# An attention stack on one core: projections moved a few slots, copies put around an exponential, splittings re-ordered

## The reference

```python
# l0: 20 heads of width 8, keys and values from ctx_2048 (512 rows of 256),
# text keys 0..76 and the remaining "ip" keys with their own weights and softmax
q = x @ Wq.T;  k, v = text @ Wk.T, text @ Wv.T;  k_ip, v_ip = ip @ Wk_ip.T, ip @ Wv_ip.T
x = (attend(q, k, v) + attend(q, k_ip, v_ip)) @ Wo.T + bo + x
# a1: self attention, 20 heads of width 64
n = layer_norm(x);  x = x + attention(n, n)
# a2: cross attention, 20 heads of width 64, here with ctx_2048 as the context
n = layer_norm(x);  x = x + attention(n, ctx_2048)
# ff
x = geglu(layer_norm(x)) + x
```

## Time and profile before

| what | value |
|---|---|
| median of 3 runs | 1513.89 us (1512.29 to 1514.84) |
| the profiled execution, its own time | 1517.58 us |
| its span, first to last instruction | 1515.8 us |
| mean granted TensorE clock | 0.997 |
| busy TensorE, VectorE, ScalarE, GpSimd | 98%, 71%, 51%, 29% |
| busy TensorE's weight loads | 77% |

### The profile page before, as it was taken

The page is one execution under the profiler, slowest core; times in us unless marked ns, Lnnn a source line. Parts: engine busy times, 40 slices in busy tenths (PEclk is TensorE's granted clock), DMA queues, the critical chain, the costliest instruction groups (busy, mean ns, idle before and its releaser), DMA issues.

```text
span 1515.8 us, 40910 instructions
## 1 busy us (share of the span) xinstructions
PE 1480.4 (98%) x17984; PEld 1168.8 (77%) x17984; DVE 1080.2 (71%) x1509; ACT 779.6 (51%) x1079; POOL 445.2 (29%) x393
## 2 busy tenths in 40 slices
PE   9999999999999999998999999999999999999999
PEld 6566566567888888887787888887888888778799
DVE  6778878866777777776677676766767677676666
ACT  4667666764554455654344444444444444443344
POOL 4433346431222223542122122222222222222210
PEclk9999999999999999999999999999999999999999
DMA  4322231300000200011010100101010030000000
GB/s 142 117 62 63 62 113 43 97 3 23 2 2 2 98 2 6 2 30 29 23 30 1 30 2 2 29 2 30 2 29 2 2 75 2 1 2 2 1 14 22
DMA packets 27212, 45.53 MB, mean 30 GB/s; under 512 B 7392, under 2 KB 15520, under 8 KB 26656
## 3 DMA queue, kind: packets, MB, share of 16 engines
q1 hardware_dynamic: 27040, 42.96, 9.7%
HBM read 29.51 MB, written 1.31 MB: 20 GB/s over the span
## 4 chain that ended last, share of the span: by engine, by line
PE 84%; ACT 5%; DVE 5%; POOL 2%; issue 1%; SPq 1%; DMA 0%; ACTq 0%; POOLq 0%; DVEq 0%
PE a_pj L1022 7%; PE a_pj L1010 6%; PE a_pj L534 5%; PE l_px L1695 5%; PE a_pv L1044 4%; PE a_px L1044 4%; PE l_pst L1593 4%; PE a_px L1062 3%; PE a_px L577 3%; PE a_pscore L950 3%; PE a_pj L543 3%; PE ff_ph L2187 3%; PE a_pst L971 2%; PE a_px L563 2%; PE a_pv L563 2%; ACT l_probs L1834 2%
## 5 line engine op out<-in xcount | busy, mean ns | idle before, releaser
L1296 POOL TENSOR_TENSOR a_key_sum<-a_probs 128x512 f32<-128x512 f32 x120 | 166.0, 1387 | 455.4 <-ACT a_probs L1121 455.4
L1203 DVE TENSOR_REDUCE a_negmax<-a_pscore 128x2 f32<-128x1024 f32 x160 | 195.5, 1222 | 94.4 <-PE a_pscore L950 94.0
L1121 ACT ACTIVATE a_probs<-a_pst 128x1024 f32<-128x1024 f32 x160 | 164.0, 1025 | 156.1 <-PE a_pst L977 155.5
L1965 DVE TENSOR_REDUCE l_negmax<-l_pscore 128x2 f32<-128x154 f32 x320 | 202.7, 684 | 49.4 <-PE l_pscore L1578 48.4
L1834 ACT ACTIVATE l_probs<-l_pst 128x1024 f32<-128x1024 f32 x160 | 164.1, 1026 | 80.7 <-PE l_pst L1593 79.8
L761 POOL TENSOR_TENSOR a_key_sum<-a_probs 128x1024 f32<-128x1024 f32 x40 | 96.8, 2421 | 223.8 <-ACT a_probs L625 223.8
L701 DVE TENSOR_REDUCE a_negmax<-a_pscore 128x4 f32<-128x1024 f32 x80 | 97.6, 1220 | 35.3 <-PE a_pscore L492 35.2
L1022 PE MATMUL a_pj<-a_wv_hi,a_ct 128*128 128x256 f32 x640 | 111.9, 287 | 1.0
L713 DVE RECIPROCAL a_recip<-a_pv 128x256 f32<-128x256 f32 x40 | 70.3, 1757 | 43.3 <-PE a_pv L568 43.3
L625 ACT ACTIVATE a_probs<-a_pst 128x1024 f32<-128x1024 f32 x80 | 81.9, 1023 | 37.2 <-PE a_pst L518 37.2
L1228 DVE RECIPROCAL a_recip<-a_pv 128x256 f32<-128x256 f32 x40 | 70.2, 1755 | 42.5 <-PE a_pv L1053 42.5
(11 more groups left out here) (259 smaller groups left out, 3638.4 us busy)
## 6 DMA issues: line engine op xcount, KB each, us to landing
l_ct<-in_ctx_t SPq DMA_DIRECT2D x8, 512.0 KB, 3.9
l_k_stack<-l_k_hi SPq DMA_DIRECT2D x64, 64.0 KB, 2.1
a_ct<-in_ctx_t SPq DMA_DIRECT2D x8, 512.0 KB, 4.6
a_ct<-in_ctx_t SPq DMA_DIRECT2D x16, 256.0 KB, 5.5
l_q_stack<-l_q_hi SPq DMA_DIRECT2D x80, 32.0 KB, 1.9
a_raw_wv<-in_a_wv SPq DMA_DIRECT2D x2, 1280.0 KB, 8.6
l_x<-in_x_t SPq DMA_DIRECT2D x8, 256.0 KB, 3.8
l_k_stack<-l_k_lo SPq DMA_DIRECT2D x32, 64.0 KB, 2.1
```

The lines of the kernel that those rows point to most:

```text
L1121: nc.scalar.activation(probs[:, 2 * i:2 * i + 2, 2 * n:2 * n + 2, :], pst[:].rearrange("p h (k q) -> p h k q", k=2), ACT.Exp, scale=SCALE) ...
L1203: nc.vector.tensor_reduce(to, pscore[:], AX.X, ALU.max, negate=True).then_inc(max_done, 1)
L1296: nc.gpsimd.tensor_tensor(key_sums[n][:, two], probs[:, two, 2 * n, :], probs[:, two, 2 * n + 1, :], ALU.add).then_inc(half_summed, 1)
L1965: last = nc.vector.tensor_reduce(to[:, :, k], pscores[s % 2][:, :, keys], AX.X, ALU.max, negate=True)
```

## The change

- EARLY: queries of batch 1 are projected in part (2, 3) and no longer (2, 1); the keys' rest in (3, 3) and no longer (2, 3). FILLED gets six matmuls at (2, 1). The fill at (3, 3) falls away, since a projection is there now.
- ScalarE: the hi copy of the keys' rest is made in the part that projects it; the lo copy stays in part 0 of the next step, behind the exponential. Both were there. This holds for all seven batches that have it.
- VectorE: a2's opening for step d-1 is called between the two parts of step d of a1, and no longer behind rest(d-1). Only openings 27 and 39 hold anything; 39 stays in its place.
- The step from a1 to a2, ScalarE: opening(39) rounds context parts 0 and 1 only; opening(40), behind the exponential of own part 0, parts 2 and 3; opening(41), behind the queries' rounding, makes sel.
- VectorE: low_context(0, 0) comes before low_queries(0), low_context(0, 1) in part 1, behind the second maximum.
- TensorE: keys(0) waits for c_ready at its first row that uses the low context (row 8, and again at 9 to 11) and no longer at row 6.

```diff
--- before.py
+++ after.py
@@ -1001,11 +1001,11 @@
                 elif u == 0:
                     pe.wait_ge(c_ready, 4 * (b + 1))
                 pe.wait_ge(q_split, d + 1)
-            if d == 0 and part == 1:
-                pe.wait_ge(c_ready, 4)
             half = len(C_ROWS) // 2
             for k in range(part * half, (part + 1) * half):
                 hw, hc, s = C_ROWS[k]
+                if d == 0 and hc == 1:
+                    pe.wait_ge(c_ready, 4)
                 for t in range(2):
                     last = mm(pj[:, t, :], wk[hw][OWN[t], s, u * P:(u + 1) * P], cts[b % 2][OWN[t], hc, s, :],
                               start=k == 0, stop=k == len(C_ROWS) - 1)
@@ -1153,13 +1153,13 @@
             if d in (33, 34):
                 act.wait_ge(loaded[2], 16)
                 copy(wv[0][:, d - 33], raws["wv"][:, d - 33]).then_inc(w_hi, 1)
-            if d == 39:
+            if d == 41:
                 for i in range(2):
                     nc.scalar.activation(sel[:, i, :], ident[:, i:i + 1].broadcast_to([P, P]), ACT.Identity,
                                          bias=ident[:, D1 + i:D1 + i + 1]).then_inc(sel_set, 1)
-            if d == 39:
-                for s in range(4):
-                    high_context(0, s)
+            if d in (39, 40):
+                for s in range(2):
+                    high_context(0, 2 * (d - 39) + s)
 
         def part(d, s):
             if here(d - 2):
@@ -1254,12 +1254,11 @@
                 if d == 1 and s == 0:
                     dve.wait_ge(negmax_zeroed, 1)
                 maximum(d - 1, s)
+            if d == 0 and s < 2:
+                low_context(0, s)
             if s == 0:
                 if here(d):
                     low_queries(d)
-            if (d, s) == (0, 1):
-                for k in range(2):
-                    low_context(0, k)
             if s == 1 and norm_at(d, LN_SPLIT):
                 ln.dve_lo(dve, norm_at(d, LN_SPLIT), nt)
             if s == 1 and d > 1 and norm_at(d, LN_STATS):
@@ -1419,8 +1418,8 @@
 
 
     EARLY = {(0, 0): ("v3", 0), (0, 1): ("ip", 1), (0, 2): ("v0", 1), (1, 0): ("v1", 1), (1, 1): ("text", 1),
-             (2, 1): ("q", 1), (2, 3): ("rest", 1), (3, 1): ("v2", 1), (4, 1): ("v3", 1)}
-    FILLED = {(0, 3): 8, (1, 2): 4, (1, 3): 8, (2, 0): 4, (2, 2): 4}
+             (2, 3): ("q", 1), (3, 1): ("v2", 1), (3, 3): ("rest", 1), (4, 1): ("v3", 1)}
+    FILLED = {(0, 3): 8, (1, 2): 4, (1, 3): 8, (2, 0): 4, (2, 1): 6, (2, 2): 4}
     PLAN = {(0, 1): "ip", (0, 3): "text", (1, 1): "q", (1, 3): "rest", (2, 3): "v0", (3, 1): "v1", (3, 3): "v2",
             (4, 1): "v3"}
 
@@ -1864,9 +1863,6 @@
                 for u in range(GROUPS):
                     wait(act, stacked[u], MOVES[u] * m)
                 pairs = [(q_n["hi"][:], q_n["lo"][:], pj[:].rearrange("p (i q) -> p i q", i=2))]
-            elif what == "rest":
-                wait(act, stacked[GROUPS - 1], MOVES[GROUPS - 1] * m)
-                pairs = [(rest_n["hi"][:], rest_n["lo"][:], pj[:])]
             elif what in ("ip", "text"):
                 for u in range(GROUPS - 1):
                     wait(act, stacked[u], MOVES[u] * (m - 1))
@@ -1879,6 +1875,15 @@
                 return
             take_values(int(what[1]), m, pj).then_inc(pj_read, 1)
 
+        def take_rest(m, half):
+
+            if half == "hi":
+                act.wait_ge(pj_ready, pj_uses["rest", m] + 1)
+                wait(act, stacked[GROUPS - 1], MOVES[GROUPS - 1] * m)
+                copy(rest_n["hi"][:], pj[:])
+            else:
+                copy(rest_n["lo"][:].bitcast(FP32), pj[:]).then_inc(pj_read, 1)
+
         def take_values(kt, m, bank):
 
             vm = vs[m % 2]
@@ -1912,8 +1917,10 @@
 
 
             if s == 0 and projected(t - 1, 3) and projected(t - 1, 3)[0] == "rest":
-                take(*projected(t - 1, 3))
-            if projected(t, s) and projected(t, s)[0] not in ("out", "s0", "rest"):
+                take_rest(projected(t - 1, 3)[1], "lo")
+            if projected(t, s) and projected(t, s)[0] == "rest":
+                take_rest(projected(t, s)[1], "hi")
+            elif projected(t, s) and projected(t, s)[0] not in ("out", "s0"):
                 take(*projected(t, s))
 
         return dict(begin=begin, part=part)
@@ -2471,7 +2478,11 @@
             cross["opening"](S1 - 1)
             for d in range(2):
                 own["part"](S1 + d, 0)
+                if d == 0:
+                    cross["opening"](S1)
                 cross["part"](d, 0)
+                if d == 0:
+                    cross["opening"](S1 + 1)
                 own["part"](S1 + d, 1)
                 for s in range(1, 4):
                     cross["part"](d, s)
@@ -2515,9 +2526,11 @@
             own["rest"](3)
             for d in range(4, S1):
                 own["part"](d, 0)
+                if d < S1 - 1:
+                    cross["opening"](d - 1)
                 own["part"](d, 1)
                 own["rest"](d)
-                cross["opening"](d)
+            cross["opening"](S1 - 1)
             for d in range(2):
                 own["part"](S1 + d, 0)
                 cross["part"](d, 0)
```

## The result

The changed kernel takes 1507.82 us (median of 8 runs, 1505.48 to 1508.77) against 1516.52 for the kernel before, timed beside it (1512.29 to 1517.82): a ratio of 0.9942, with a 95% interval of 0.9932 to 0.9953. That is 8.7 us won, where 8.0 were forecast.

A forecast was written before the change was run, and what follows sets the result against it. TensorE, busy 98%, was taken as the bound, so only its idle or low-clock time could change. Terms -2.4 - 1.35 - 5.1 + 0.7 = -8.15, say -8.0 us, from median 1513.89 gave 1505.9; range 1502.9 to 1510.6.

The forecast's parts named there:

- second and third gap: TensorE idle: 1.35 us at 592.62 for a maximum; 1.14 then 2.73 us at the step from a1 to a2.
- first gap: First layer's step 2: TensorE idle 2.12 us before the turning of the maxima, then some 6 us at half speed.
- Part 1: Keys' rest, one copy before and one after the exponential: five waits and a sixth change, 2.4 us won.
- Part 2: VectorE's low rows of wq behind a1's first maximum: the 1.35 us gap closes; bounds 1.1 and 1.55.
- Part 3: Step from a1 to a2: idle and low clock go, queries wait longer; 5.1 us won if VectorE precedes GpSimd.
- The rival order: At the a1 to a2 step, GpSimd's key sum starts before VectorE's second context subtraction; about 2.3 us won, chance 0.30.
- Part 4: New slots for queries, rest and fills in the first steps: new wait at step 5, 0.7 us net cost.
- Cover 1.2: At step 5's first projection, only 1.2 us of the slots' gain counts, since GpSimd's split ends near 56.5.
- Price 1.9: Clock falls again behind the new wait of about 2.3 us at step 5, costing 1.9 us.
- B: GpSimd ahead of VectorE at the a1 to a2 step: -5.35 us, 1508.5; chance 0.30.
- C: Slots cost 1.8, copies win 1.2, wq move 1.1, GpSimd ahead: -2.8 us, 1511.1; chance 0.17.
- D: Hi copy waits for each batch's last stack, delaying exponentials: slower, 1514 to 1518 us; chance 0.03.

The follow-up runs named there:

- p4_slots: Kernel before with only the new slots of the first steps (queries, keys' rest, fills); 1517.27 us, span 1515.5.
- p1_halves: Kernel before with only the hi copy of the keys' rest moved into the part that projects it; 1514.28 us, span 1512.5.
- p2_wq: Kernel before with only VectorE's opening of the next layer moved between the two parts of a1's step; 1514.70 us, span 1512.9.
- b_xs_last: Kernel before with the xs loads and three small loads moved behind the second batch's last stack; 1517.39 us, span 1515.6.
- a_xs_later: Changed kernel with the eight xs loads and three small loads moved behind the second batch's third stack; span 1508.6 us.
- after_again: Changed kernel unaltered, timed again as reference for the moved loads; 1507.39 us, ratio 0.9937 to the kernel before, span 1504.4.
- a_fill20: Changed kernel with 20 useless matmuls in front of step 5's first projection, where TensorE waited for GpSimd; span 1505.6 us.
- a_key_sum_first: Changed kernel with GpSimd's memset behind its key sum, so the sum starts ahead of VectorE's second context subtraction; span 1506.9 us.

## Why the prediction was right, step by step

- **What bounds.** Right. To within 0.3 us, all that was won lies in TensorE's second and third gap, the copies' waits and the stretch of low clock behind the third gap; what the first gap gave was spent again at step 5.
- **Part 1, predicted -2.4.** Measured -2.5 in the change, -2.7 alone. The hi copy found the idle time in front of the exponential; L1739's wait is gone. TensorE's lead grew by 0.30 us at the change that is followed by fills (forecast 0.24) and by 0.46 to 0.50 at each of the other five (0.45); 0.2 of it was lost again near 300 us, in the change only.
- **Part 2, predicted -1.35.** -1.6 from a1's first projection to a2's queries, in the change (377.1 us to 375.5) and alone (375.5). The 0.25 beyond the gap of 1.35 has no row that explains it. The 1.5 us more that it brought alone is the hidden price of the clock and not part 2's.
- **Part 3, predicted -5.1.** -5.1 both ways, and in the forecast order: VectorE 0.24 us ahead of GpSimd, against 0.15 rolled. The wait for the queries was 0.93 us, forecast 0.8. The rival order was overpriced: 1.9 us, measured, against 5.1 - 2.3 = 2.8. It charged a wait of 2.2 us, which was 1.63, and clock as well, but the clock held. One reading behind this part was wrong: low_queries, 0.69 us, was taken as a subtraction with GpSimd silent, but GpSimd's pair of 2.52 us from 706.33 was under way at 708.21. One input of low_queries lies in PSUM, those of low_context both in SBUF. The price taken from it, 0.6 to 0.7 us, held all the same: low_context alone, at 701.76, took 0.68.
- **Part 4, predicted +0.7.** The mechanism was right at each point (first gap gone, the new wait for GpSimd, the fall behind it), and the sum was not: -0.07 in the change, -0.2 alone, which is within the scatter of the kernels with the old slots (61.18 to 61.91), and up to -2.3 in other executions of the new slots. "Cover 1.2" was 57.70 - 56.16 = 1.5; TensorE arrived at 53.1 and not 54.1, which only lengthened the wait (3.05 instead of 2.3; in `p4_slots`, without part 1, it was 2.30). "Price 1.9" was 5.68 - 4.21 = 1.5, by the distance from the rest projection to the text projection, 4.21 before. Together 0.8 of mis-sizing in the first trace.
- **The sum.** -8.15 predicted, -9.3 in the spans: 0.8 from part 4, 0.25 from part 2, the rest of part 1. By the medians -8.7, and the forecast 1505.9 lies 1.9 us below the 1507.82 although it forecast 0.7 us too little won: it was taken from the median of three runs, 1513.89, where eight gave 1516.52. The base was 2.6 us too low and the gain 0.7 too small, and these two errors work against each other, so the forecast time is 0.7 us nearer than it deserves by luck.
- **Rivals.** B and C fall with the order at the transition. D did not occur: no exponential waits for a transfer behind a hi copy.

What stays open: why the clock fell in the opening of two of the thirteen traces. TensorE was busy before and during it, so no wait in these traces explains it. And why stacks land earlier or later from one execution to the next was not tried: GpSimd let step 5's projection go at 54.8 us in one trace and at 56.5 in another, with the same loads in front of the stacks.

## What to carry to other kernels

Removing a wait moves TensorE's arrival at the next one: before adding up, list who is late next, and follow that engine's list back to the queue that feeds it. Here 2.95 us more, by the medians, lay in the order of SyncE's loads, and that order was worth nothing without the new slots. When two engines share a port, the order of their starts, 0.1 us apart, decides about 2 us; here a memset of 0.5 us in front of GpSimd's sum holds the good order, and such cheap work can be placed for it. Compare kernels that differ by 1 us by distances between landmarks on either side of the edit, since the span of one execution carries 1 to 2 us from elsewhere.

## What the runs showed of the hardware

- Each time the granted clock fell, the low level lasted one of two times by the stretches. It was 3.4 us at step 5 in four kernels, at the transition in before, p1_halves, p2_wq, p4_slots and b_xs_last, and in the opening in two. It was 6.8 to 6.9 us behind the first gap in all five kernels with the old slots (in before 0.84, 0.50 and 0.81 in the three 4 us stretches from 32 to 44) and behind the 3.90 us wait of a_xs_later.
- Waits of 1.11, 1.35 and 1.63 us were not followed by a fall; those of 1.81 and 1.92 (the first gap in p1_halves and b_xs_last) and all longer ones, up to 3.90, were. The length of the single wait doesn't decide alone: in p2_wq the fall came behind one of 1.14 us, and two came in the opening with no wait at all (after_again and a_fill20, 24 to 32).
- A VectorE subtraction of 128x512 with one input in PSUM took 0.69 us while GpSimd's pair of subtractions ran (before, after). With both inputs in SBUF it took 0.68 us alone, and 2.79 us when begun 0.13 us behind GpSimd's key sum (a_key_sum_first).
- 3.4 us of low clock cost 1.4 to 1.6 us where TensorE was the bound, and nothing that shows where the slow work lay in front of a wait (p2_wq).
